# Token lists of a gated MoE kernel: list values from two broadcast instructions a group, and the shared expert's add to X moved ahead of the low halves

## The chip, the cores and the metric

The kernel runs on one core of a Trainium2 chip. A core has five engines that run their own instruction streams and meet only at semaphores: TensorE (PE in the profile, its weight loads PEld), VectorE (DVE), ScalarE (ACT), GpSimd (POOL), and SyncE (SP), which here only issues DMAs. The metric is the device time of one execution in microseconds; lower is better. Before the change it is 693.31 us, the median of three runs (689.36, 693.31 and 694.84).

## The reference, cut to what matters

```python
x = x + tanh(g_xattn[0]) * (0.6 * sigmoid(si + sj + b) + 0.4 * layernorm(x))   # si, sj from ctx_512
h = layernorm(x)                                     # 2048 tokens of 512
probs = softmax(h @ gate_w.T)                        # 16 experts
vals, idx = top_k(probs, 4)                          # each token goes to 4 experts
w = vals / sum(vals)
act = silu(h @ w_gate[e]) * (h @ w_up[e])            # fp4 codes times scales, 512 -> 2 x 384
out = sum over the 4 experts of w[e] * (act @ w_down[e])      # 384 -> 512
out = out + shared expert's (swiglu, down) on every token
x = x + tanh(g_ffn[0]) * out
```

## The kernel before, in words

The 2048 tokens are 16 tiles of 128 (NT = 16). The program has three stages. In the first the attention-like part, the two layer norms and the transposes make `xT`, the normalised tokens in two f16 halves. In the second, which lasts from about 45 to 186 us, the shared expert runs over the 16 tiles, one **shared slot** per tile, and beside it the routing is worked out. In the third the 16 routed experts run over lists of tokens that are gathered by indirect DMA, and the results are added to the output by indirect DMA.

**One shared slot i.** PE multiplies tile i by the gate and up weights in two halves of 12 matmuls (`gate_up`, L1203); between them it transposes the activations of slot i-1 (`transpose_act`, L1217); then it multiplies those by the down weights (`down`, L1231, 9 matmuls, slot i-1). ACT applies silu (L613) when both halves of slot i are there. DVE multiplies gate and up (`activations`, L989). ACT rounds the result to f16 (the high half, L620). DVE subtracts that from the f32 result (the low half, `low_halves`, L994); PE's next `transpose_act` waits for both halves. `add_y` (L998) adds the down result of slot i-1 from PSUM to X and frees that PSUM bank; it waits for `down(i-1)`. After that DVE does the slot's share of other work (`after_shared_slot`, L1029): dequantisation of the first routed expert (slots 5 to 8, L908 to L931), the routing (`route`, slot 9), ranks and positions (slot 10), token weights (slot 11), the lists (slots 11 and 12, `mark`), `lists` (slot 13), tables (slot 14), and the rest of the first routed expert's dequantisation (slot 15), which begins with the tick of L948 that lets PE start the first routed slot.

**The lists.** A token's j-th choice (j = 0 to 3) has a position in the list of its expert: a row (0 to 127) and a slot (0 to 79, since SLOTS = 80). `mark(j)` builds two f16 operands. `onehot` [128 tokens, 128 rows, 16 tiles] is 1 where the row matches, from one instruction of 2048 elements a partition (L1026). `values` [128 tokens, 16 tiles, 80 slots] is token number + 1 where the slot matches, and 0 elsewhere, from 16 instructions of 80 elements (L1023), one for each tile: compare `slot_h` (0 to 79) with the token's slot, multiply by the token's number. `list_tokens(j)` on PE then multiplies the two, 16 matmuls for each j, with `onehot[:, j % 2, :, i]` as the weights and the tile's `values` as the moving operand of 80 columns (L1258). All 64 matmuls add up in one PSUM bank. `values` and `onehot` have two buffers, so `mark(2)` waits for the end of `list_tokens(0)`, and `mark(3)` for that of `list_tokens(1)`.

**Order.** Every engine's order is that of the code. On PE the four `list_tokens` stand after `down(11)` (j = 0, 1) and after `down(12)` (j = 2, 3); behind them stand `gate_up(13)` and `gate_up(14)`. POOL makes constants at the start (L411 to L431), then helps with the layer norms, makes `place` (L489), and is idle until the lists are done.

Of the kernel before, what the change touches and what calls it, by code (L numbers as in the profile page):

```python
# [6 lines left out]
F32, F16 = mybir.dt.float32, mybir.dt.float16  # L7
I32, U16 = mybir.dt.int32, mybir.dt.uint16
ALU = mybir.AluOpType
# [3 lines left out]
P = 128  # L13
LN_EPS = 1e-5
P_ASEM = 0.6
TOP_K = 4
# [13 lines left out]
def gated_xattn_moe(nc, x, ctx_512, g_xattn, g_ffn, xattn_w, xattn_b, gate_w, gu_packed, gu_scales,  # L30
# [6 lines left out]
    NT = B * S // P  # L37
# [11 lines left out]
    SLOTS = T * TOP_K // P + E  # L49
# [15 lines left out]
    with ExitStack() as ctx:  # L65
        def sb(name, shape, dt):
            return ctx.enter_context(nc.sbuf_tensor(name, shape, dt))
# [4 lines left out]
        def sem(name):  # L72
# [80 lines left out]

        onehot = room_a[:, :].bitcast(F16).rearrange("p (b q i) -> p b q i", b=2, i=NT)
        values = mix_room[:, 1:3].rearrange("p k b h -> p (k b h)").bitcast(F16)[:, 0:2 * SLOTS * NT]\
            .rearrange("p (b i s) -> p b i s", b=2, i=NT)
        place = spare.rearrange("p b h -> p (b h)").bitcast(F16).rearrange("p (q i) -> p q i", i=NT)
        xg = room_b[:, 0:2 * ROW].rearrange("p (b n) -> p b n", b=2)
        at = [2 * ROW]
# [16 lines left out]
        rank = wide[:, E * NT:2 * E * NT].rearrange("p (e i) -> p e i", i=NT)  # L176
        g_pos = wide[:, 2 * E * NT:3 * E * NT].rearrange("p (i e) -> p i e", e=E)
        pos_i = sb("pos_i", [P, 3, TOP_K, NT], I32)
        pos_slot = sb("pos_slot", [P, TOP_K, NT], F32)
        pos_row = sb("pos_row", [P, TOP_K, NT], F16)  # L180
        start_f = sb("start_f", [P, E], F32)
        tri = sb("tri", [P, P], F16)
        ones16 = sb("ones16", [P, P], F16)
        sel16 = sb("sel16", [P, NT * E], F16)
        sel = sel16[:, :].rearrange("p (t e) -> p t e", e=E)
        token1 = sb("token1", [P, NT], F32)
        dump_row = sb("dump_row", [P, 1], F32)


# [7 lines left out]
        first_tiles_i = sb("first_tiles_i", [P, E], I32)  # L197
        pairs_i = sb("pairs_i", [P, 1], I32)
        slot_f = sb("slot_f", [P, SLOTS], F32)
        slot_h = sb("slot_h", [P, SLOTS], F16)  # L200
        before_s = sb("before_s", [P, SLOTS], F32)
        first_of_expert = sb("first_of_expert", [P, SLOTS], F32)
        slot_i = sb("slot_i", [P, SLOTS], I32)
# [122 lines left out]

            return 16 * LOADS * (n // 2 + 1)

        POOL_CONST = 16


        LEAD = 8
# [77 lines left out]
        def _(pool):  # L410
# [7 lines left out]
            nc.gpsimd.memset(ones16[:, :], 1.0).then_inc(pool_const, 1)  # L418
            for dst, pattern, base, mult in ((token1[:, :], [[P, NT]], 1, 1), (dump_row[:, :], [[0, 1]], DUMP + 1, 1),
                                             (iota_s[:, :], [[1, SLOTS]], 0, 0),  # L420
                                             (before_s[:, :], [[16, SLOTS // 2], [16, 2]], 0, 0),
                                             (slot_h[:, :], [[1, SLOTS]], 0, 0)):
                nc.gpsimd.iota(dst, pattern, base=base, channel_multiplier=mult,
                               allow_small_or_imprecise_dtypes=True).then_inc(pool_const, 1)
            pool.wait_ge(pool_const, 13)

            nc.gpsimd.affine_select(out=tri[:, :], in_=tri[:, :], compare_op=ALU.is_gt, fill=-1.0, base=0,
                                    pattern=[[1, P]], channel_multiplier=-1).then_inc(pool_const, 1)
            for ident in (id32, id16):
                nc.gpsimd.affine_select(out=ident[:, :], in_=ident[:, :], compare_op=ALU.not_equal, fill=1.0,  # L430
                                        base=0, pattern=[[-1, P]], channel_multiplier=1).then_inc(pool_const, 1)  # L431

            def inverse_std(k, b):

# [259 lines left out]
        def _(v):  # L694
# [289 lines left out]
            def activations(s, b, weight):  # L984

                if not isinstance(s, int) or s >= 2:
                    v.wait_ge(at_done, s - 1)
                v.wait_ge(sg_done, s + 1)
                nc.vector.scalar_tensor_tensor(act[:, b, :], gu_ps[:, 2 + b, 0:I], weight, sg[:, b, :], ALU.mult,  # L989
                                               ALU.mult).then_inc(act_done, 1)  # L990

            def low_halves(s, b):
                v.wait_ge(ah_done, s + 1)
                nc.vector.tensor_tensor(acth[:, b, 1, :], act[:, b, :], acth[:, b, 0, :], ALU.subtract).then_inc(al_done, 1)  # L994
# [18 lines left out]
            def mark(j):  # L1013

                if j >= 2:
                    v.wait_ge(list_ready, j - 1)
                else:
                    v.wait_ge(place_ready, 1)
                    for k in range(ROWS_AHEAD):
                        v.wait_ge(st_rows[k], 16 * (NT // ROWS_AHEAD))  # L1020

                for i in range(NT):
                    mm = nc.vector.tensor_scalar(values[:, j % 2, i, :], slot_h[:, :], pos_slot[:, j, i:i + 1], token1[:, i:i + 1],  # L1023
                                                 ALU.is_equal, ALU.mult)
                mm.then_inc(values_ready, 1)
                nc.vector.tensor_tensor(onehot[:, j % 2], pos_row[:, j, :].unsqueeze(1).broadcast_to([P, P, NT]), place,  # L1026
                                        ALU.is_equal).then_inc(onehot_ready, 1)

            def after_shared_slot(i):  # L1029

# [51 lines left out]
            second_stats(1)  # L1082
            for i in range(2, NT):
                activations(i, i % 2, shared_w[:, 0:1])
                low_halves(i, i % 2)
                add_y(i - 1)
                after_shared_slot(i)

            def head(r, e):
# [54 lines left out]
        def _(pe):  # L1144
# [108 lines left out]
            def list_tokens(j):  # L1253

                pe.wait_ge(onehot_ready, j + 1)
                pe.wait_ge(values_ready, j + 1)
                for i in range(NT):
                    mm = nc.tensor.matmul(rt_ps[:, 0:SLOTS], onehot[:, j % 2, :, i], values[:, j % 2, i, :],  # L1258
                                          start=(j == 0 and i == 0), stop=(j == TOP_K - 1 and i == NT - 1))
                mm.then_inc(list_ready, 1)  # L1260

# [103 lines left out]
```

## Time and profile before

| | |
|---|---|
| three timed runs | 689.36, 693.31, 694.84 us (median 693.31) |
| profiled execution, first to last instruction (span) | 689.3 us; this is the only time recorded for it |
| PE busy | 622.6 us (90%) |
| PE weight loads busy | 375.9 us (55%) |
| DVE busy | 496.2 us (72%) |
| ACT busy | 325.8 us (47%) |
| POOL busy | 327.7 us (48%) |
| mean granted TensorE clock | 0.98 of full speed |

The busy shares are means over stages with different limits. The page cuts the span into 40 slices of 17.2 us; PE's busy digits lie between 3 and 9 in the first thirteen slices, and are 9 (90% or more) in all later ones but the last. DVE's digits are 8 or 9 in the slices from 86.2 to 172.3 us, the end of which is the stretch in which the lists are made. A chain of waits is read from its end backwards: each piece was released by the one before it.

### The profile page before, as it was taken

Reading aid. Unit: us, or ns where it says so; the run is one execution under the profiler, and the core shown is the slowest. Engines: PE = TensorE matmul, PEld = TensorE weight load, DVE = VectorE, ACT = ScalarE, POOL = GpSimd, SP = SyncE. Lnnn points to the kernel's source line nnn. Section 1 sums busy time; section 2 is a strip of 40 time slices with the busy share of each in tenths; the row PEclk is TensorE's granted clock in tenths of the full one; section 3 lists DMA queues with packets and bytes.
Section 4 is the critical chain, followed back from the end, with each engine's and each line's share of the span. In section 5 each row is a group of like instructions: output and inputs, shape, how many; then the busy total and the mean of one; then the engine's idle time right before and its main releaser. Section 6 shows DMA issues by size and latency. Waiting matters only on the chain.

```text
span 689.3 us, 17258 instructions
## 1 busy us (share of the span) xinstructions
PE 622.6 (90%) x4394; PEld 375.9 (55%) x4395; DVE 496.2 (72%) x1271; ACT 325.8 (47%) x558; POOL 327.7 (48%) x506
## 2 busy tenths in 40 slices
PE   3668869887898999999999999999999999999992
PEld 2444545444554656565555656566565655656550
DVE  5878788989776858588777867688588878867210
ACT  1763577231343554454544455454554545455441
POOL 2521844000235456564646565564655656565432
PEclk9999989998999999999999999999999999999996
DMA  8670111128156875857577684848767587654432
GB/s 235 203 241 1 63 46 70 40 53 276 49 162 152 207 179 118 189 115 189 107 196 174 128 215 82 225 78 204 177 127 186 117 193 174 141 89 68 90 47 31
DMA packets 49841, 93.72 MB, mean 136 GB/s; under 512 B 8840, under 2 KB 16776, under 8 KB 49816
## 3 DMA queue, kind: packets, MB, share of 16 engines
q0 software_dynamic: 16128, 38.35, 30.1%
q1 hardware_dynamic: 32936, 55.04, 27.1%
q8 instruction: 11, 0.18, 0.1%
q10 hardware_dynamic: 752, 0.04, 0.1%
q14 instruction: 14, 0.11, 0.1%
HBM read 65.16 MB, written 28.24 MB: 135 GB/s over the span
## 4 chain that ended last, share of the span: by engine, by line
PE 72%; DVE 13%; ACT 4%; DMA 3%; issue 3%; POOL 2%; SPq 1%; DVEq 0%; POOLq 0%; ACTq 0%
PE gu_ps L1203 41%; PE bank L1231 20%; PE bank L1243 4%; PE bank L1217 4%; DVE mix_room L1023 2%; DMA dn_sc<-dn_scale_halves 2%; DVE act L989 1%; DMA room_a<-in_ctx 1%; ACT acth L620 1%; PE gu_ps L1163 1%; DVE X L998 1%; PE bank L1160 1%; DVE acth L994 1%; DVE dn_code L920 1%; ACT mix_room L579 1%
## 5 line engine op out<-in xcount | busy, mean ns | idle before, releaser
L1203 PE MATMUL gu_ps<-wgu,mix_room 128*128 x1728 | 304.4, 326 | 3.3 <-DVE tick L948 2.1
L1203 PEld LDWEIGHTS gu_ps<-wgu,mix_room 128*128 128x128 f16 x1728 | 166.0, 98 | 114.5 <-issue 7.4
L1231 PE MATMUL bank<-wdn,aT 128*128 (+1 forms) x792 | 186.5, 381 | 4.2 <-ACT aT L627 3.7
L528 POOL DMA_INDIRECT out<-mix_room,idx_s x72 | 123.9, 1721 | 31.9 <-issue 30.5
L627 ACT ACTIVATE aT<-bank 128x768 f16<-128x768 f16 x88 | 71.2, 810 | 130.9 <-PE bank L1217 126.0
L1231 PEld LDWEIGHTS bank<-wdn,aT 128*128 128x128 f16 x792 | 77.6, 98 | 89.5 <-issue 3.2
L989 DVE SCALAR_TENSOR_TENSOR act<-gu_ps,wslot,sg x72 | 44.5, 618 | 96.2 <-ACT sg L613 79.4
L499 POOL TENSOR_TENSOR pool_tick<-ones 128x1 f32<-128x1 f32 x144 | 36.0, 250 | 162.7 <-DMA out<-mix_room,idx_s 79.6
L620 ACT ACTIVATE acth<-act 128x384 f16<-128x384 f32 x88 | 46.0, 523 | 135.8 <-DVE act L989 131.4
L510 POOL DMA_INDIRECT room_b<-token_rows,idx_g x72 | 76.5, 1063 | 12.1 <-issue 3.7
L994 DVE TENSOR_TENSOR acth<-act,acth (+1 forms) x88 | 49.2, 560 | 38.1 <-ACT acth L620 37.6
L507 POOL COPY idx_g<-room_b 128x1 int32 (+1 forms) x72 | 41.8, 581 | 70.9 <-DVE tick L859 51.3
L638 ACT ACTIVATE mix_room<-bank 128x1024 f16<-128x1024 f16 x72 | 73.2, 1017 | 0.3 <-PE bank L1243 0.3
L925 DVE TENSOR_TENSOR wgu<-dq_code,gu_sc 128x768 f16<-128x768 f16 x136 | 70.8, 561 | 2.3
L1203 PE MATMUL gu_ps<-wgu,xT 128*128 128x384 f16 x384 | 71.5, 340 | 0.0
L613 ACT ACTIVATE sg<-gu_ps 128x384 f32<-128x384 f32 x88 | 43.2, 491 | 57.3 <-PE gu_ps L1203 55.0
L1217 PE MATMUL bank<-id,acth 128*128 128x128 f16 x528 | 44.0, 219 | 10.7 <-ACT acth L620 8.7
L1203 PEld LDWEIGHTS gu_ps<-wgu,xT 128*128 128x128 f16 x384 | 37.4, 101 | 25.5 <-issue 5.0
L1217 PEld LDWEIGHTS bank<-id,acth 128*128 128x128 f16 x528 | 36.1, 98 | 25.4 <-ACT acth L620 13.8
L931 DVE TENSOR_TENSOR wdn<-dn_code,dn_sc 128x384 f16<-128x384 f16 x136 | 43.6, 362 | 0.7
L1243 PE MATMUL bank<-id,room_b 128*128 128x128 f16 x576 | 43.9, 219 | 0.0
L644 ACT ACTIVATE mix_room<-bank 128x512 f32<-128x512 f32 x72 | 41.8, 580 | 4.2 <-PE bank L1231 4.2
(156 smaller groups left out, 586.2 us busy)
## 6 DMA issues: line engine op xcount, KB each, us to landing
dn_sc<-dn_scale_halves SPq DMA_DIRECT2D x34, 384.0 KB
dn_raw<-in_L_ffn_down_packed SPq DMA_DIRECT2D x48, 256.0 KB
gu_sc<-gu_scale_halves SPq DMA_DIRECT2D x34, 192.0 KB
X<-in_x SPq DMA_DIRECT2D x4, 1024.0 KB, 8.1
token_rows<-room_a SPq DMA_DIRECT2D x16, 256.0 KB, 2.3
out<-X SPq DMA_DIRECT2D x4, 1024.0 KB, 10.6
gu_raw<-in_L_ffn_gate_up_packed SPq DMA_DIRECT2D x16, 192.0 KB
gu_raw<-in_L_ffn_gate_up_packed SPq DMA_DIRECT2D x16, 191.9 KB
```

The lines of the kernel that those rows point to most:

```text
L510: nc.gpsimd.indirect_dma_start(xg[:, b, :], None, rows_dram[:, :], bass.IndirectOffsetOnAxis(idx_g[:, b:b + 1], 0)).then_inc(xg_ld[b], 16)
L528: nc.gpsimd.indirect_dma_start(out[:, :], bass.IndirectOffsetOnAxis(idx_s[:, b:b + 1], 0), y_sb[:, b, :], None, compute_op=ALU.add).then_i ...
L620: nc.scalar.activation(acth[:, b, 0, :], act[:, b, :], ACT.Copy).then_inc(ah_done, 1)
L627: nc.scalar.activation(aT[:, b].rearrange("p a c t -> p (a c t)"), at_ps, ACT.Copy).then_inc(aT_done, 1)
L638: nc.scalar.activation(xTs[:, b, :], xT_ps, ACT.Copy).then_inc(xTs_done, 1)
L925: link(nc.vector.tensor_tensor(wgu[:, buf, hl, c, :], dq_code[:, :], gu_sc[:, buf, hl, :], ALU.mult), wait=False)
L989: nc.vector.scalar_tensor_tensor(act[:, b, :], gu_ps[:, 2 + b, 0:I], weight, sg[:, b, :], ALU.mult, ALU.mult).then_inc(act_done, 1)
L994: nc.vector.tensor_tensor(acth[:, b, 1, :], act[:, b, :], acth[:, b, 0, :], ALU.subtract).then_inc(al_done, 1)
L1203: mm = nc.tensor.matmul(ps[b][:, 0:I], x(xp * HC + c), wgu[:, w, wp, c, col:col + I], start=(c == 0 and xp == 0 and wp == 0), stop=(c == H ...
L1217: mm = nc.tensor.transpose(at_ps[:, k * P:(k + 1) * P], acth[:, b, hl, t * P:(t + 1) * P], id16[:, :])
L1231: mm = nc.tensor.matmul(y_ps[0 if shared else b][:, :], aT[:, b, ap, t, :], wdn[:, w, wp, t, :], start=(n == 0), stop=(n == 3 * IC - 1))
L1243: mm = nc.tensor.transpose(xT_ps[:, k * P:(k + 1) * P], chunk_h(halves[:, k // HC, :], k % HC), id16[:, :])
```

## The change

Three things change. First, `values` is laid out as [tokens, slots, tiles] in place of [tokens, tiles, slots], and is built by two wide instructions on DVE in place of 16 narrow ones: a compare of 1280 elements a partition (`pos_slot` broadcast over the slots against a constant `slot_place`), then `onehot` as before, then a multiply of 1280 elements in place by `token1` broadcast over the slots. All operands are f16; `pos_slot` and `token1` were f32. The multiply is now what signals `values_ready`. Second, POOL makes the constant `slot_place` (1280 elements a partition) once, behind its other constants, in place of `slot_h` (80 elements); the first `mark` waits for it too. Third, in shared slots 2 to 15 `add_y(i - 1)` stands between `activations(i)` and `low_halves(i)`, where it stood behind `low_halves(i)`. PE's matmuls of the lists are the same in number and shape, but a moving operand `values[:, j % 2, :, i]` now takes every 16th f16 element (32 bytes apart), where it took 80 neighbours.

```diff
--- before.py
+++ after.py
@@ -153,7 +153,7 @@
 
         onehot = room_a[:, :].bitcast(F16).rearrange("p (b q i) -> p b q i", b=2, i=NT)
         values = mix_room[:, 1:3].rearrange("p k b h -> p (k b h)").bitcast(F16)[:, 0:2 * SLOTS * NT]\
-            .rearrange("p (b i s) -> p b i s", b=2, i=NT)
+            .rearrange("p (b s i) -> p b s i", b=2, i=NT)
         place = spare.rearrange("p b h -> p (b h)").bitcast(F16).rearrange("p (q i) -> p q i", i=NT)
         xg = room_b[:, 0:2 * ROW].rearrange("p (b n) -> p b n", b=2)
         at = [2 * ROW]
@@ -176,14 +176,15 @@
         rank = wide[:, E * NT:2 * E * NT].rearrange("p (e i) -> p e i", i=NT)
         g_pos = wide[:, 2 * E * NT:3 * E * NT].rearrange("p (i e) -> p i e", e=E)
         pos_i = sb("pos_i", [P, 3, TOP_K, NT], I32)
-        pos_slot = sb("pos_slot", [P, TOP_K, NT], F32)
+        pos_slot = sb("pos_slot", [P, TOP_K, NT], F16)
+        slot_place = sb("slot_place", [P, SLOTS, NT], F16)
         pos_row = sb("pos_row", [P, TOP_K, NT], F16)
         start_f = sb("start_f", [P, E], F32)
         tri = sb("tri", [P, P], F16)
         ones16 = sb("ones16", [P, P], F16)
         sel16 = sb("sel16", [P, NT * E], F16)
         sel = sel16[:, :].rearrange("p (t e) -> p t e", e=E)
-        token1 = sb("token1", [P, NT], F32)
+        token1 = sb("token1", [P, NT], F16)
         dump_row = sb("dump_row", [P, 1], F32)
 
 
@@ -197,7 +198,6 @@
         first_tiles_i = sb("first_tiles_i", [P, E], I32)
         pairs_i = sb("pairs_i", [P, 1], I32)
         slot_f = sb("slot_f", [P, SLOTS], F32)
-        slot_h = sb("slot_h", [P, SLOTS], F16)
         before_s = sb("before_s", [P, SLOTS], F32)
         first_of_expert = sb("first_of_expert", [P, SLOTS], F32)
         slot_i = sb("slot_i", [P, SLOTS], I32)
@@ -326,7 +326,7 @@
 
             return 16 * LOADS * (n // 2 + 1)
 
-        POOL_CONST = 16
+        POOL_CONST = 15
 
 
         LEAD = 8
@@ -418,17 +418,19 @@
             nc.gpsimd.memset(ones16[:, :], 1.0).then_inc(pool_const, 1)
             for dst, pattern, base, mult in ((token1[:, :], [[P, NT]], 1, 1), (dump_row[:, :], [[0, 1]], DUMP + 1, 1),
                                              (iota_s[:, :], [[1, SLOTS]], 0, 0),
-                                             (before_s[:, :], [[16, SLOTS // 2], [16, 2]], 0, 0),
-                                             (slot_h[:, :], [[1, SLOTS]], 0, 0)):
+                                             (before_s[:, :], [[16, SLOTS // 2], [16, 2]], 0, 0)):
                 nc.gpsimd.iota(dst, pattern, base=base, channel_multiplier=mult,
                                allow_small_or_imprecise_dtypes=True).then_inc(pool_const, 1)
-            pool.wait_ge(pool_const, 13)
+            pool.wait_ge(pool_const, 12)
 
             nc.gpsimd.affine_select(out=tri[:, :], in_=tri[:, :], compare_op=ALU.is_gt, fill=-1.0, base=0,
                                     pattern=[[1, P]], channel_multiplier=-1).then_inc(pool_const, 1)
             for ident in (id32, id16):
                 nc.gpsimd.affine_select(out=ident[:, :], in_=ident[:, :], compare_op=ALU.not_equal, fill=1.0,
                                         base=0, pattern=[[-1, P]], channel_multiplier=1).then_inc(pool_const, 1)
+
+            nc.gpsimd.iota(slot_place[:, :, :], [[1, SLOTS], [0, NT]], base=0, channel_multiplier=0,
+                           allow_small_or_imprecise_dtypes=True).then_inc(place_ready, 1)
 
             def inverse_std(k, b):
 
@@ -1015,16 +1017,18 @@
                 if j >= 2:
                     v.wait_ge(list_ready, j - 1)
                 else:
-                    v.wait_ge(place_ready, 1)
+                    v.wait_ge(place_ready, 2)
                     for k in range(ROWS_AHEAD):
                         v.wait_ge(st_rows[k], 16 * (NT // ROWS_AHEAD))
 
-                for i in range(NT):
-                    mm = nc.vector.tensor_scalar(values[:, j % 2, i, :], slot_h[:, :], pos_slot[:, j, i:i + 1], token1[:, i:i + 1],
-                                                 ALU.is_equal, ALU.mult)
-                mm.then_inc(values_ready, 1)
+                by_slot = [P, SLOTS, NT]
+                step(nc.vector.tensor_tensor(values[:, j % 2], pos_slot[:, j, :].unsqueeze(1).broadcast_to(by_slot),
+                                             slot_place[:, :, :], ALU.is_equal), wait=False)
                 nc.vector.tensor_tensor(onehot[:, j % 2], pos_row[:, j, :].unsqueeze(1).broadcast_to([P, P, NT]), place,
                                         ALU.is_equal).then_inc(onehot_ready, 1)
+                v.wait_ge(vs, count[0])
+                nc.vector.tensor_tensor(values[:, j % 2], token1[:, :].unsqueeze(1).broadcast_to(by_slot), values[:, j % 2],
+                                        ALU.mult).then_inc(values_ready, 1)
 
             def after_shared_slot(i):
 
@@ -1082,8 +1086,8 @@
             second_stats(1)
             for i in range(2, NT):
                 activations(i, i % 2, shared_w[:, 0:1])
+                add_y(i - 1)
                 low_halves(i, i % 2)
-                add_y(i - 1)
                 after_shared_slot(i)
 
             def head(r, e):
@@ -1255,7 +1259,7 @@
                 pe.wait_ge(onehot_ready, j + 1)
                 pe.wait_ge(values_ready, j + 1)
                 for i in range(NT):
-                    mm = nc.tensor.matmul(rt_ps[:, 0:SLOTS], onehot[:, j % 2, :, i], values[:, j % 2, i, :],
+                    mm = nc.tensor.matmul(rt_ps[:, 0:SLOTS], onehot[:, j % 2, :, i], values[:, j % 2, :, i],
                                           start=(j == 0 and i == 0), stop=(j == TOP_K - 1 and i == NT - 1))
                 mm.then_inc(list_ready, 1)
 
```

DVE's order around slot 11, where the first two lists are made, was this (`mix_room` holds `values` and `place`, `room_a` holds `onehot`, `acth` the two halves, `X<-bank` is `add_y`):

```order
L989 SCALAR_TENSOR_TENSOR act<-gu_ps,shared_w,sg 128x384
L994 TENSOR_TENSOR acth<-act,acth 128x384
L998 SCALAR_TENSOR_TENSOR X<-bank,X 128x512
L788 TENSOR_TENSOR r_exp<-r_exp,sel 128x256
L789 TENSOR_REDUCE r_sum<-r_exp 128x16
L790 RECIPROCAL r_sum<-r_sum 128x16
L792 TENSOR_SCALAR r_sum<-r_sum,shared_w 128x16
L793 TENSOR_TENSOR cw<-r_exp,r_sum 128x256
L1023 TENSOR_SCALAR mix_room<-slot_h,pos_slot,token 128x80 x16
L1026 TENSOR_TENSOR room_a<-pos_row,mix_room 128x2048
```

In the changed program, whose lines are numbered two to four higher there, the same place reads:

```order
L991 SCALAR_TENSOR_TENSOR act<-gu_ps,shared_w,sg 128x384
L1000 SCALAR_TENSOR_TENSOR X<-bank,X 128x512
L996 TENSOR_TENSOR acth<-act,acth 128x384
L790 TENSOR_TENSOR r_exp<-r_exp,sel 128x256
L791 TENSOR_REDUCE r_sum<-r_exp 128x16
L792 RECIPROCAL r_sum<-r_sum 128x16
L794 TENSOR_SCALAR r_sum<-r_sum,shared_w 128x16
L795 TENSOR_TENSOR cw<-r_exp,r_sum 128x256
L1025 TENSOR_TENSOR mix_room<-pos_slot,slot_place 128x1280
L1027 TENSOR_TENSOR room_a<-pos_row,mix_room 128x2048
L1030 TENSOR_TENSOR mix_room<-token,mix_room 128x1280
```

The add to X moved ahead of the low half, 16 narrow instructions became one ahead of `onehot` and one behind it, and the last of the three is now the multiply; the same three stand for each of the four j.

On POOL, at the end of its constants and ahead of its first work for a layer norm (`rstd`), the program before had:

```order
L423 IOTA before_s 128x80
L423 IOTA slot_h 128x80
L427 AFFINE_SELECT tri<-tri 128x128
L430 AFFINE_SELECT id<-id 128x128 x2
L437 TENSOR_TENSOR rstd<-veps,mhalf 128x4
```

and the changed one has:

```order
L422 IOTA before_s 128x80
L426 AFFINE_SELECT tri<-tri 128x128
L429 AFFINE_SELECT id<-id 128x128 x2
L432 IOTA slot_place 128x1280
L439 TENSOR_TENSOR rstd<-veps,mhalf 128x4
```

The small `slot_h` went, and the wide `slot_place` stands behind the last constant that another engine waits for.

## Rows read from the trace of the kernel before

**Rows 1.** The page, chain that ended last: shares of the span by engine
```profile
PE 72%; DVE 13%; ACT 4%; DMA 3%; issue 3%; POOL 2%; SPq 1%; DVEq 0%; POOLq 0%; ACTq 0%
```

**Rows 2.** Stretches: length; PE, PEld, DVE, ACT, POOL busy; PE clock; DMA share; GB/s
```profile
149.00:157.00 8.00, 3.99 (x31) 2.25 (x28) 7.95 (x33) 0.49 (x1) 0.00 (x0) 1.00 0.72 166
157.00:164.00 7.00, 5.21 (x33) 3.14 (x33) 6.41 (x22) 0.53 (x1) 0.00 (x0) 0.51 0.96 297
```

**Rows 3.** Chain of waits, 145 to 190 us: start, length, what
```profile
161.01 3.37 DVE mix_room L1023 x16
164.38 1.13 DVE room_a L1026
...
170.07 1.19 PE bank L1258 x16
171.26 1.95 PE gu_ps L1203 x12
...
186.16 2.12 PE gu_ps L1203 x12
```

**Rows 4.** Timeline of DVE: start, length, instruction, count, idle before and its releaser
```profile
119.54 2.65 DVE L920 TENSOR_SCALAR dn_code<-dn_bits 128x384 f16<-128x384 f16 x1
...
128.49 1.03 DVE L925 TENSOR_TENSOR wgu<-dq_code,gu_sc 128x768 f16<-128x768 f16 x2
...
146.75 0.56 DVE L994 TENSOR_TENSOR acth<-act,acth 128x384 f16<-128x384 f32 x1 [0.59 <-ACT acth L620]
147.23 0.68 DVE L998 SCALAR_TENSOR_TENSOR X<-bank,X 128x512 f32<-128x512 f32 x1
...
149.63 3.46 DVE L1023 TENSOR_SCALAR mix_room<-slot_h,pos_slot,token 128x80 f16<-128x80 f16 x16
...
176.13 0.62 DVE L989 SCALAR_TENSOR_TENSOR act<-gu_ps,shared_w,sg 128x384 f32<-128x384 f32 x1 [3.00 <-ACT sg L613]
...
179.50 1.49 DVE L841 TENSOR_TENSOR room_b<-iota_s,cum_f 128x1280 f16<-128x1280 f32 x1
```

**Rows 5.** Timeline of PE, slots 10 to 14
```profile
137.63 0.62 PE L1249 MATMUL bank<-sel,tri 128*128 128x256 f16 x1 [1.30 <-DVE sel L782]
138.07 0.64 PE L1250 MATMUL bank<-sel,ones 128*128 128x256 f16 x1
138.53 2.13 PE L1203 MATMUL gu_ps<-wgu,xT 128*128 128x384 f16 x12
...
149.69 2.10 PE L1231 MATMUL bank<-wdn,aT 128*128 128x512 f16 x9
154.28 1.19 PE L1258 MATMUL bank<-mix_room,room_a 128*128 128x80 f16 x16 [2.48 <-DVE room_a L1026]
158.79 1.28 PE L1258 MATMUL bank<-mix_room,room_a 128*128 128x80 f16 x16 [3.32 <-DVE room_a L1026]
159.87 4.04 PE L1203 MATMUL gu_ps<-wgu,xT 128*128 128x384 f16 x12
...
175.33 2.11 PE L1231 MATMUL bank<-wdn,aT 128*128 128x512 f16 x9
```

**Rows 6.** Weight loads of lines L1258 and L1249: ns min/median/max, first and last start
```profile
L1258 PEld LDWEIGHTS bank<-mix_room,room_a x64: 140/164/178, 154.3 to 171.0; 128*128 128x128 f16 x64
L1249 PEld LDWEIGHTS bank<-sel,tri x1: 95/95/95, 137.6 to 137.6; 128*128 128x128 f16 x1
```

**Rows 7.** Timeline of POOL
```profile
14.64 1.06 POOL L437 TENSOR_TENSOR rstd<-veps,mhalf 128x4 f32<-128x4 f32 x1 [10.70 <-DVE veps L726]
...
119.36 2.62 POOL L489 IOTA mix_room<- 128x2048 f16 x1
```

**Rows 8.** Chain of waits, 74 to 90 us
```profile
76.95 0.60 DVE X L998
...
78.28 4.60 POOL X L443 x4
```

**Rows 9.** Chain of waits, 195 to 222 us
```profile
204.83 11.53 DMA dn_sc<-dn_scale_halves
```

## The prediction

> **What bounds the kernel now.** I read the chain of waits first. Over the span PE carries 72% of it and DVE 13% [rows 1]; the reader is to see where those 13% lie, since nothing that the change edits is PE's own work. Between 145 and 190 us the chain runs on DVE through the narrow instructions of the lists and `onehot` (16 take 3.37 us, then 1.13), and reaches PE only behind the last list at 170.07 [rows 3]. The stretches agree: from 149 to 157 us DVE is busy 7.95 of 8.00 us and PE 3.99 [rows 2]. DVE's timeline shows the other idle time: in a shared slot it waits 0.59 us for ACT's high half ahead of the low half [rows 4]. After 175.33 the chain is `gate_up(14)`, then DVE's tables and the tick that lets PE begin the first routed slot at 186.16 [rows 3, 5]. What the change gains or loses must show in that start; whatever moves it moves the rest of the program with it.
>
> **Before the lists: `add_y` ahead of the low half.** The wait of 0.59 us is filled by an add of 0.60 (147.23 in [rows 4], less overlap), provided that `down(i-1)` is done. Then DVE leaves a slot about 0.6 us earlier, while the low half ends where it did. This counts only where DVE sets the pace, which is in slots 7 to 11 and 15 (by slot 14 it waits 3.00 us for PE). In slot 7, dequantisation behind it is held up by POOL: an instruction there lasts 2.65 from 119.54, while POOL makes `place` from 119.36 to 121.98 [rows 4, 7]. I count 0.2 of its 0.6. Slots 8, 9, 10 and 11 count 0.6 each. In slot 3 the add is on the chain too (76.95), ahead of the layer norm's factors and POOL's work from 78.28 [rows 8]; there `down(2)` ends late, and I take 0.4. Slots 2, 4, 5 and 6 wait for PE or POOL next, and count nothing. So the low half of slot 11 comes 0.4 + 0.2 + 3 x 0.6 = 2.4 us earlier, and the first `mark` 3.0 us earlier (0.6 of slot 11 more).
>
> **The lists on DVE.** The trace has no compare of 1280 elements with these operands. `onehot` has the same form (f16, one operand broadcast over the middle dimension), and takes 1.13 us for 2048 [rows 3]; a plain f16 multiply of 768 takes 1.03 - 0.56 = 0.47 [rows 4]. The line through both is 0.07 + 0.516 ns an element, so 0.73 us for 1280. The bounds are 0.70 (1280/2048 of `onehot`) and 1.50 (an f32 operand, 179.50 [rows 4]); 0.73 is taken, since the types are `onehot`'s. A `mark` becomes 0.73 + 1.13 + 0.73 = 2.60 us against 3.37 + 1.13 = 4.50, which is 1.9 less, 7.6 for four. The wait between compare and multiply is covered by `onehot`, which is between them.
>
> **The lists on PE.** These matmuls took 68 ns each (158.79 to 159.87, 16 of them [rows 5]). That is about the weight load: on L1258, whose weights lie 32 bytes apart, it lasts 164 ns against 95 for neighbouring ones [rows 6]. The 80 neighbouring columns hid behind it. Now these lie 32 bytes apart too. One place of the trace streams such an operand, L1249 and L1250, whose moving `sel` has that step: 256 columns take 0.44 and 0.46 us from start to start [rows 5], or 1.72 to 1.80 ns a column, at full clock. A plain stream of 384 columns takes 1.95/12 us, 0.42 ns a column [rows 3]. So 80 columns cost 138 to 144 ns, and with a start of a few ns I take 142 ns, 2.27 us a list. Bounds: 1.08 as now, and 16 x (142 + 68) = 3.4 if weight load and stream add up.
>
> The Trainium skill speaks against the new layout here: "SBUF — State Buffer", section "Door 1: The DMA port swizzle", has lines of 16 bytes and a penalty for each access that goes to a new line, which every column now does; the slow `sel` agrees. The Trainium skill's "TensorE: Matmul & The Clock Gate", section "Part 2: What happens when you issue a matmul", gives weights and stream a read port each; by that the 3.4 would not occur.
>
> **The sum.** A row of PE's timeline has a pipeline tail of 0.17 us (2.13 against 1.95 for the same 12 matmuls [rows 3, 5]), which is left out here. PE ended `down(11)` at 149.69 + 2.10 - 0.17 = 151.62, and now does so 2.4 earlier, at 149.2, since the slot's transposes waited for the low half. `mark(0)` runs from 146.6 to 149.2, so list 0 takes PE from 149.4 to 151.7; `mark(1)` ends at 151.8, list 1 takes from 151.9 to 154.2. From here PE is the one that is waited for: `gate_up(13)` with its transposes takes 175.33 - (171.26 - 0.17) = 4.24, as `gate_up(14)` does there, `down(12)` 1.94, lists 2 and 3 take 4.54, `gate_up(14)` again 4.24, and ends at 169.15. Marks 2 and 3 end by 156.2 and 158.8 and delay nothing. Before, `gate_up(14)` ended at 175.33 [rows 5]: **6.2 us earlier**. Of 7.6 us that DVE saves in the lists, and 3.0 ahead of them, 4.4 is given back because PE becomes the bound and its lists are 4.8 us longer. In slot 14 the add must wait for `down(13)`, so the low half and the tables come 0.2 later after the activation than before; slot 15 gains its 0.6, as `down(14)` is done by then. **6.2 - 0.2 + 0.6 = 6.6 us**; the first routed slot starts at 179.6.
>
> At nothing I cost: `slot_place` on POOL, some 1.7 us by 2.62 x 1280/2048, under an idle stretch of 10.70 us that ends at 14.64 [rows 7]; with that cover gone it would cost the 1.7. Nor do I cost the f16 forms of `pos_slot` and `token1`, made by the instructions that made them in f32. The gather of the first routed rows keeps its lead, since `lists`, which it waits for, comes 7 us earlier too. Nothing behind 186 us gains by itself. The next wait there, 11.53 us for a scale load [rows 9], hangs on a store behind the last `add_y`, in expert 0's stream, and moves along.
>
> The profiled execution has 689.3 us and becomes 682.7. It is 0.6% below the median of the timed runs, which spread by 5.5 us. Against the median the forecast is 693.3 - 6.6 = **686.7 us**.
>
> **The rivals.**
>
> *The strided stream costs nothing* (0.10). Lists stay at 1.1 us: list 1 ends at 153.0, `down(12)` at 159.2, list 3 at 161.4, `gate_up(14)` at 165.7. That is 9.6 and with slots 14 and 15 10.0 us, so 683.3. For it: the matmuls are short and wait on weights anyway. Against it: `sel` at 1.75 ns a column. The Trainium skill's "TensorE: Matmul & The Clock Gate", section "Back-to-back issue gap", lets the gap grow with the column count alone, and would give this case; the `sel` rows disagree with it.
>
> *Stream and weight load add up* (0.13). Lists of 3.4 us cost 4 x 1.13 more, less 0.3 that PE waited ahead of list 1: 6.6 - 4.2 = 2.4 us gain, 690.9. For it is that both would then read with long steps at once; the rows of `sel`, whose weights are neighbours, do not tell.
>
> *The clock falls in the lists* (0.12). Before, PE idled ahead of lists 0 and 1 (2.48 and 3.32 us), the clock was at 0.51 from 157 to 164 us, the lower of 1.2 and 2.4 GHz, and a half of `gate_up(13)` took 4.04 instead of 1.95 us [rows 2, 5]. DVE hid that then. If it falls again behind lists 0 and 1, 2.0 us of it now lie on PE's path: 4.6 us gain, 688.7. Against it: the idle times are down to 0.2.
>
> *The broadcast instructions run no faster than the f32 form* (0.03): 1.50 us each, a `mark` 4.13. List 1 then starts 3.1 us later and PE's path behind it with it, for a gain of 3.5 and 689.8. Against it: `onehot`.
>
> *Slower* (0.04). The stream and the clock meet: at the lower clock the strided columns cost twice 1.75 ns, 280 ns, and add the weight load's 68, 5.6 us a list. Four lists cost 4 x 3.3 = 13.2 more than I take, against 6.6: slower by 6.6, and with the half of `gate_up(13)` by 8.6, about 702. It decides from 3.9 us a list on. Against it: at the lower clock list 1 took 1.28 us against list 0's 1.19 [rows 5], so strided reads hardly follow that clock.
>
> **How the numbers follow.** The forecast has 0.58. A measurement tells about 1% of this kernel, 6.9 us, from no change, and the forecast of 6.6 lies just inside, so the spread of the runs splits it: 0.32 of the 0.58 faster by more, as the median shown is above the profiled execution and the lowest run and may fall back, 0.25 within, 0.01 slower. The free stream adds 0.09 faster, the clock 0.03, the rest 0.01, together 0.45; the slow case leaves 0.03 slower, 0.04 in all; 0.51 are within. The range takes in the free stream with 1.9 us of run spread below it, and the adding stream above: 681.5 to 691.
>
> **What the changed profile would show.** Compare and multiply of 1280 at 0.73 us from start to start; 16 list matmuls in 2.3 us; no idle time of 0.59 ahead of the low half in slots 7 to 11; `gate_up(13)` at full clock; PE's first routed slot at 179.6 us, and its distance to the end unchanged at 503.1 us. Wrong I am if list matmuls keep to 68 ns or go above 200, if the clock falls under `gate_up(13)`, or if the distance to the end changes.

## The result: 5% slower, and the loss lies where the prediction said nothing changes

The changed kernel took 725.75 us (median of 6, 722.01 to 730.66) against 691.38 us for the kernel before (median of 6: the three runs of the table and three more): a ratio of 1.0497, 95% interval 1.0455 to 1.0539. The forecast was 686.7 us and its range ended at 691. The profiled execution took 722.01 us, its span is 720.2 us; the prediction made the span 682.7. The 37.5 us between the two split at the first routed slot. PE starts it at 185.14 us where 179.6 was forecast (5.5 us), and from there to the end are 535.1 us where 503.1 was forecast (32.0 us).

**The lists.** Below is PE's timeline of the changed kernel (start, time, engine, line, operation, tiles, shapes, count, idle time before it), with rows in between left out. It answers to [rows 5]:

```profile
149.06 2.10 PE L1235 MATMUL bank<-wdn,aT 128*128 128x512 f16 x9
151.24 5.24 PE L1262 MATMUL bank<-mix_room,room_a 128*128 128x80 f16 x32
156.30 3.61 PE L1207 MATMUL gu_ps<-wgu,xT 128*128 128x384 f16 x12
163.98 5.05 PE L1262 MATMUL bank<-mix_room,room_a 128*128 128x80 f16 x32
168.84 3.34 PE L1207 MATMUL gu_ps<-wgu,xT 128*128 128x384 f16 x12
174.77 2.11 PE L1235 MATMUL bank<-wdn,aT 128*128 128x512 f16 x9
185.14 2.12 PE L1207 MATMUL gu_ps<-wgu,mix_room 128*128 x12 [1.64 <-DVE tick L950]
```

From start to start the two pairs of lists take 5.06 and 4.86 us, so 158 and 152 ns a matmul. PE no longer waits for DVE ahead of them, but the first half of `gate_up` behind each pair takes 3.61 and 3.34 us instead of the 2.11 of full clock; the kernel before lost that behind its first pair (4.04 [rows 5]), and not behind its second (2.12 from 171.09). The stretches of the same run give the clock (busy us and count of each engine, granted clock, DMA share, GB/s); they answer to [rows 2]:

```profile
149.00:157.00 8.00, 7.93 (x46) 5.76 (x44) 8.00 (x11) 1.02 (x2) 0.00 (x0) 0.93 0.83 197
157.00:164.00 7.00, 7.00 (x39) 3.75 (x38) 4.21 (x6) 1.81 (x3) 0.00 (x0) 0.83 1.00 366
164.00:169.00 5.00, 5.00 (x34) 4.77 (x33) 1.16 (x2) 0.02 (x1) 0.00 (x0) 1.00 0.72 281
169.00:176.00 7.00, 7.00 (x37) 3.96 (x35) 1.23 (x5) 1.30 (x2) 3.04 (x6) 0.76 0.35 96
```

The granted clock falls behind both pairs, to the lower of its two levels for a part of the stretch, although PE was busy for 26.93 of these 27 us.

DVE's side went as forecast. Its timeline:

```profile
148.40 0.82 DVE L1025 TENSOR_TENSOR mix_room<-pos_slot,slot_place 128x1280 f16<-128x1280 f16 x1
149.14 1.22 DVE L1027 TENSOR_TENSOR room_a<-pos_row,mix_room 128x2048 f16<-128x2048 f16 x1
150.27 0.82 DVE L1030 TENSOR_TENSOR mix_room<-token,mix_room 128x1280 f16<-128x1280 f16 x1
151.01 0.82 DVE L1025 TENSOR_TENSOR mix_room<-pos_slot,slot_place 128x1280 f16<-128x1280 f16 x1
```

Compare and multiply take 0.74 us from start to start, a `mark` 151.01 - 148.40 = 2.61 us.

**The routed stage.** The change edits nothing there, and yet DVE's loop over pairs of experts (a `Fori` of six passes) now stops at each of its five jumps back. This is the chain of waits of the changed kernel around the first stop (start, us, what, with small pieces left out; "issue" is time in which the engine waited for nothing that the profile shows, and DVEq is DVE's sequencer):

```profile
315.99 0.55 DVE wgu L927
316.54 3.71 issue
320.25 0.07 DVEq L1141
320.36 0.33 DVEq L1106
321.13 0.05 issue
321.84 0.63 DVE act L991
322.49 0.53 ACT acth L622
323.86 0.80 PE bank L1221 x6
```

L1141 is the loop itself: the last multiply of a pass is done at 316.54, and the jump back to the loop's first instruction shows only at 320.25. The next activation waits, ACT waits for it, and PE waits for ACT. The chain has five such pieces, 3.71, 3.33, 5.69, 6.32 and 4.25 us, at 316.54, 376.27, 447.31, 513.64 and 576.96. DVE's idle time ahead of the activation behind them is 5.30, 4.91, 7.29, 7.91 and 5.84, together 31.25 us. At the same five jumps the kernel before has 1.02, 1.22, 1.86, 1.72 and 1.21, together 7.03; this is its first:

```profile
317.85 0.62 DVE L989 SCALAR_TENSOR_TENSOR act<-gu_ps,wslot,sg  x1 [1.02 <-issue]
```

So DVE's idle time grew by 24.2 of the 32.0 us. The other 7.8 are not split by a run, but the stretches say where they can lie: PE idles during a stop, and in the 6 to 8 us behind the five stops the granted clock is 0.79, 0.60, 0.72, 0.51 and 0.55, where it is 1.00 behind all five jumps of the kernel before. These are the 8 us behind the first stop, in the changed kernel and then in the kernel before:

```profile
322.00:330.00 8.00, 6.14 (x36) 3.85 (x37) 6.08 (x16) 3.62 (x7) 3.93 (x6) 0.79 0.82 197
```

```profile
322.00:330.00 8.00, 8.00 (x55) 4.63 (x54) 6.55 (x17) 3.88 (x8) 2.46 (x7) 1.00 0.77 195
```

The page has one more difference, in the DMA queue that brings instructions (packets, MB, share of the engines' span), here of the changed kernel and then of the kernel before:

```profile
q14 instruction: 39, 0.32, 0.1%
```

```profile
q14 instruction: 14, 0.11, 0.1%
```

The extra 25 packets, five for each jump, are the only hint on the page at what DVE waits for. The trace says more, stretch by stretch: exactly one packet of this queue falls into each of the five stops, and in the kernel before none at all falls between 303 and 620 us, in which its five jumps lie.

### The profile page after: what moved, and what is told of

Its sections match the earlier page's. It is cut to its first block, busy times and chain, and to the rows that moved or that the text cites. A ratio compares the mean times of both kernels' runs of the same rounds, so it can differ in the third digit from the quotient of the medians.

```text
span 720.2 us, 17202 instructions
## 1 busy us (share of the span) xinstructions
PE 639.7 (89%) x4394; PEld 387.4 (54%) x4395; DVE 488.1 (68%) x1215; ACT 325.8 (45%) x558; POOL 326.1 (45%) x506
## 4 chain that ended last, share of the span: by engine, by line
PE 69%; DVE 10%; issue 7%; ACT 4%; DMA 3%; POOL 2%; DVEq 2%; SPq 1%; ACTq 0%; POOLq 0%
PE gu_ps L1207 38%; PE bank L1235 18%; PE bank L1247 4%; PE bank L1221 4%; DMA dn_sc<-dn_scale_halves 2%; DVE act L991 2%; PE bank L1262 1%; ACT acth L622 1%; DMA room_a<-in_ctx 1%; PE gu_ps L1167 1%; POOL room_a L462 1%; PE bank L1164 1%; PE bank L1191 1%; DVE wgu L927 1%; DVEq L991 1%
## 5 line engine op out<-in xcount | busy, mean ns | idle before, releaser
L1207 PE MATMUL gu_ps<-wgu,mix_room 128*128 x1728 | 310.6, 330 | 2.6 <-DVE tick L950 1.6
L1207 PEld LDWEIGHTS gu_ps<-wgu,mix_room 128*128 128x128 f16 x1728 | 168.3, 99 | 117.5 <-issue 12.3
L1221 PE MATMUL bank<-id,acth 128*128 128x128 f16 x528 | 45.7, 225 | 32.8 <-ACT acth L622 31.0
L1207 PE MATMUL gu_ps<-wgu,xT 128*128 128x384 f16 x384 | 74.1, 348 | 0.0
L509 POOL COPY idx_g<-room_b 128x1 int32 (+1 forms) x72 | 37.4, 520 | 68.9 <-DVE tick L861 47.1
L1247 PE MATMUL bank<-id,room_b 128*128 128x128 f16 x576 | 46.2, 225 | 0.0
```

The lines of the kernel that those rows point to most:

```text
L1207: mm = nc.tensor.matmul(ps[b][:, 0:I], x(xp * HC + c), wgu[:, w, wp, c, col:col + I], start=(c == 0 and xp == 0 and wp == 0), stop=(c == H ...
L1221: mm = nc.tensor.transpose(at_ps[:, k * P:(k + 1) * P], acth[:, b, hl, t * P:(t + 1) * P], id16[:, :])
L1247: mm = nc.tensor.transpose(xT_ps[:, k * P:(k + 1) * P], chunk_h(halves[:, k // HC, :], k % HC), id16[:, :])
```

## The experiments

Theory 1: the change took 56 instructions out of DVE's program ahead of the loop (16 narrow ones became 2 wide ones, four times; the page counts 1271 and now 1215), so the loop lies at another place of the code, and the jump back now leads to code that must be fetched again. Theory 2: the moved add, the strided lists or the data's timing slow the routed stage. The kernel has a knob that moves DVE's code: `LEAD` small memsets at the start of DVE's program, 8 of them, while DVE waits for the scales. Their tile is the last that is laid out, so no other tile's address moves with it. Each ratio below is to executions of the kernel before that were timed beside the run.

**1. The changed kernel with the 56 instructions put back as memsets.**

```diff
-        LEAD = 8
+        LEAD = 64
```

> The changed kernel with 64 instead of 8 small memsets at the start of VectorE's program, in the time in which it waits for the scales (8 of them took 0.26 us, so 56 more are 1.8 us inside an idle 4.9 us). From the marks on, every VectorE instruction of the program then stands at the same place of the code as in the kernel before, because the change took 56 instructions out ahead of it. Theory 1 (the place of VectorE's expert loop in its code costs the 32 us): no issue pieces of 3 us or more in the chain, first routed slot at about 185 us, from there to the end 503 us (kernel before) and not 535, time 688 to 692. Theory 2 (the order of the add to X, the strided lists or the later data slow the routed stage): the 535 us stay, time 722 to 728. If part of each, something between.

Measured: 689.98 us, ratio to the kernel before 0.9976 (0.9954 to 0.9997). First routed slot at 184.47 us, 504.0 us from there, 14 packets. The whole loss of the routed stage is gone with nothing of the change's own work undone: theory 1 holds, theory 2 falls.

**2. The kernel before with its loop moved to where the change puts it** (`LEAD = 208`; 200 more is 56 fewer modulo 256).

> The kernel before with 208 instead of 8 memsets at VectorE's start: 200 more instructions, which is 56 fewer modulo 256, and nothing else. Theory 1 with blocks of 256 instructions: the expert loop falls across its blocks as in the changed kernel, the routed stage goes from 503 to about 535 us, and the memsets end about 2 us after the scales landed, so 720 to 727 us, with issue pieces of 3 to 6 us at the loop's back edge. Theory 2: only the late start, 691 to 694 us, no such pieces. Theory 1 with another period than 256 could give either; then a second point would be needed.

Measured: 728.64 us, 1.0562 (1.0512 to 1.0611); 538.9 us behind the first routed slot, 41 packets, the five pieces in the chain again (3.00 to 6.14 us). The loss needs nothing of the change but the place.

**3. The kernel before with 256 more** (`LEAD = 264`), against the doubt that it is the number of memsets.

> The kernel before with 264 memsets at VectorE's start, 256 more than it has, beside the run with 200 more that took 728 us. If the place counts modulo 256 instructions, the routed stage is back at 503 us with about 14 packets of the instruction queue, and the time is 690 plus 3 to 4 us of late start: 692 to 696 us. If it is the number of memsets or the later start that cost the 38 us of the run with 200 more, 730 us or above.

Measured: 692.91 us, 1.0017 (0.9993 to 1.0041); 503.5 us behind the first routed slot, 16 packets. A place 256 instructions further is as free as the old one; more memsets than in run 2 cost nothing but the later start (first routed slot 191.08, in a profiled execution that was the slowest of the eight).

**4. Half the padding** (`LEAD = 36` in the changed kernel).

> The changed kernel with 36 memsets at VectorE's start: halfway between the changed kernel (8, routed stage 535 us) and the run with 64 (504 us). By the theory of the code's place there is one edge between them and the time is one of the two, 725 or 690 us, with 39 or 14 packets of the instruction queue; a cost that falls with the number of instructions would give some 707 us.

Measured: 747.75 us, 1.0816 (1.0771 to 1.0862), which neither expectation had: 563.2 us behind the first routed slot. Its chain shows why (small pieces left out):

```profile
315.65 4.94 issue
320.59 0.07 DVEq L1141
320.70 0.33 DVEq L1106
321.37 0.11 DVEq L1095
321.47 5.62 issue
327.09 0.05 DVEq L989
```

Each pass has two stops: one at the jump, and a second 5 instructions later (L1141, three of L1106, L1095), between L1095 and L989. I read it so: the loop's first 5 instructions lie at the very end of one piece of code, and the next piece has to come too. In the changed kernel, with 28 memsets fewer, 33 instructions lie ahead of that edge, and no second stop shows. With pieces of 128, which run 5 suggests and run 6 tests, this gives the edge's place: the loop's start is 123 instructions into a piece of 128 here, by which it is at 95 in the changed kernel and at 23 in the kernel before.

**5. Sixty further than the good place** (on the kernel of run 9, which stands at 23 too; `LEAD = 124`).

> The kernel with groups of 4 tiles with 124 memsets instead of 64 at VectorE's start, 60 more instructions ahead of the loop. The kernel before stood less than 28 instructions from the place where the loop begins to cost (the run with 36 memsets took 748 us); if the loop only has to lie inside two blocks of 256, its 332 instructions leave 180 places that are all alike, and 60 further on the routed stage is 501 to 505 us as at 64, about 14 packets of the instruction queue, time 683 to 687. If each place has its own price, the routed stage moves by several us either way.

Measured: 719.5 us, 1.0420 (1.0388 to 1.0452); 538.3 us behind the first routed slot, 40 packets, five pieces in the chain of 3.13 to 6.92 us. My first form of theory 1, that the loop must only lie inside two blocks of 256, fell here. The instruction queue's packets (0.32 MB in 39, 8.2 KB each) suggested smaller pieces. The Trainium skill's "Runtime: NRT & Kernel Launch", section "Instruction fetch mechanics", has 256 instructions in 16 KiB, by which a packet would hold 128, an estimate.

**6 and 7. Two models of the pieces** (`LEAD = 192` and `LEAD = 88` on the same kernel).

> The kernel with groups of 4 tiles with 192 memsets, 128 more than the run of 684.5 us; the run with 60 more took 719.5 us, so that lying inside two blocks of 256 instructions is not enough. Model H: the code is held in pieces of 128 instructions (the instruction queue's packets are about 8 KB), four of them, one ahead of the running one; the jump back costs when its target lies more than two pieces behind. Then 128 more instructions change nothing: routed stage 501 to 505 us, about 14 packets, time 684 to 688 with a start that is up to 2 us later. Model B: blocks of 256, the next one fetched from halfway on, so that the jump back costs when it stands in the second half of a block: 128 more put it there, routed stage about 535 us, time 718 to 724.

> The kernel with groups of 4 tiles with 88 memsets, 24 more than the run of 684.5 us and 36 fewer than the run of 719.5. In the run with 36 memsets the second stall comes 5 instructions behind the loop's start, which sets the piece's edge there; by it the loop's start is at 23 of its piece of 128 at 64 memsets, at 47 here, and the jump back 331 instructions later is still in the third piece (47 + 331 = 378, below 384). By both models no loss: 683 to 687 us, about 14 packets. If the edge was read wrongly: about 719.

Measured: 682.89 us, 0.9900 (0.9858 to 0.9941), 501.4 us behind the first routed slot, 15 packets; and 685.77 us, 0.9936 (0.9848 to 1.0023), 505.2 us, 15 packets. Model H held, model B fell. Five packets a jump fit it as well: the changed kernel's loop reaches over four pieces (95 + 331 = 426), and one is fetched ahead of the running one; in the kernel before, whose loop reaches over three, nothing was fetched again. DVE's timeline at the start of the run with 192 memsets shows the same 128: it pauses after 60 memsets, and again after 128 more.

```profile
0.86 1.72 DVE L707 MEMSET lead<- 128x1 f16 x60 [0.71 <-PEq L1358]
2.98 3.63 DVE L707 MEMSET lead<- 128x1 f16 x128 [0.40 <-issue]
7.14 0.15 DVE L707 MEMSET lead<- 128x1 f16 x4 [0.53 <-issue]
```

All places together. The loop has 332 instructions in the compiled program (the traces have only those that ran), the jump is 331 behind its start, and by model H it is free while start + 331 stays below 3 x 128 = 384:

| place of the loop's start in its piece | + 331 | runs | behind the first routed slot, us |
|---|---|---|---|
| 23 | 354 | kernel before, runs 1, 3, 6, 8 to 12 | 501.4 to 505.7 |
| 47 | 378 | run 7 | 505.2 |
| 83 | 414 | run 5 | 538.3 |
| 95 | 426 | changed kernel, run 2 | 535.1, 538.9 |
| 123 | 454 | run 4 | 563.2 |

The same section of the Trainium skill's "Runtime: NRT & Kernel Launch" says that a taken branch to a target outside the window of two pages of 256 instructions stops the engine for a fetch. The kind of stop is what the traces show; the size of the window differs. Whichever of the edges found here begins a page of 256, either the changed kernel's loop or run 5's would lie within two pages, and both stop at each jump. The measurement decides: three pieces of 128 fit all runs here, with the limit itself seen only as between 378 and 414.

**8. The moved add alone** (on the kernel before).

```diff
-                low_halves(i, i % 2)
                 add_y(i - 1)
+                low_halves(i, i % 2)
```

> The kernel before with the shared slots' add to X moved between the activations and their low part, nothing else; VectorE's number of instructions and the places of its loop do not change. My sum for this part alone was 3.0 us at the first mark; the changed kernel's trace showed waits of 0.72 us for the down product in five slots, so 0 to 3 us here: first routed slot 183 to 186.5 us, time 688 to 692. Theory 1: from the first routed slot to the end 503 us. Theory 2 in the form that the order of the add slows the routed stage: 520 us or more, time above 705.

Measured: 688.22 us, 0.9962 (0.9940 to 0.9984): 2.6 us of gain by the ratio (1.1 to 4.1). First routed slot at 180.86 in a profiled execution that was the fastest of ten.

**9. The change with a step of 8 bytes on PE**: values in four groups of 4 tiles, the same two wide instructions.

```diff
-            .rearrange("p (b s i) -> p b s i", b=2, i=NT)
+            .rearrange("p (b g s i) -> p b g s i", b=2, g=NT // 4, i=4)
...
-                    mm = nc.tensor.matmul(rt_ps[:, 0:SLOTS], onehot[:, j % 2, :, i], values[:, j % 2, :, i],
+                    mm = nc.tensor.matmul(rt_ps[:, 0:SLOTS], onehot[:, j % 2, :, i], values[:, j % 2, i // 4, :, i % 4],
```

(`LEAD = 64`; the broadcast views of the two instructions follow the layout, and `slot_place` keeps 4 columns a slot.)

> The run with 64 memsets and the moved add, with the list values laid out in four groups of 4 tiles, slot by slot inside a group, so that TensorE's moving operand steps 4 values (8 bytes) and not 16 (32 bytes); the same two wide VectorE instructions. If the step of the moving operand is what makes a list matmul take 155 ns: 68 to 80 ns each as in the kernel before, the lists then wait for the marks (2.61 us each), the pairs end about 1.3 and 2.7 us earlier, and the clock after them holds better; first routed slot at 178 to 181 us against 184.5, time 683 to 687. If the weight load (140 to 178 ns, unchanged here) sets the pace once VectorE no longer does, the matmuls stay at 140 to 165 ns, first routed slot at 184 to 185 us, time about 690. If the wide instructions lose VectorE's speed with 4 values in a row: marks of 3.5 us or more and no gain.

Measured: 684.46 us, 0.9906 (0.9879 to 0.9933), the fastest here but for run 6, which was executed twice. PE's timeline, with rows in between left out:

```profile
152.40 1.42 PE L1262 MATMUL bank<-mix_room,room_a 128*128 128x80 f16 x16
155.01 1.44 PE L1262 MATMUL bank<-mix_room,room_a 128*128 128x80 f16 x16 [1.19 <-DVE mix_room L1030]
156.28 2.13 PE L1207 MATMUL gu_ps<-wgu,xT 128*128 128x384 f16 x12
162.47 2.69 PE L1262 MATMUL bank<-mix_room,room_a 128*128 128x80 f16 x32
164.98 2.13 PE L1207 MATMUL gu_ps<-wgu,xT 128*128 128x384 f16 x12
179.60 2.12 PE L1207 MATMUL gu_ps<-wgu,mix_room 128*128 x12 [1.63 <-DVE tick L950]
```

From start to start 32 matmuls take 2.51 us, 78 ns each, and both halves of `gate_up` behind the lists run at full clock (granted 1.00 from 149 to 187 us). That full clock does not come with the layout: with the same lists the half behind the first pair took 3.81, 3.81 and 4.02 us in the profiled executions of runs 5, 7 and 12, and 2.13 in run 6's. Behind the second pair it took 2.13 in all five. DVE's wide instructions stay at 0.82 us. Weights with their step of 32 bytes are as in the changed kernel, so it was the moving operand that set its pace.

**10. The same with groups of 8 tiles**, a step of 16 bytes.

> As the kernel with groups of 4, with two groups of 8 tiles: the moving operand steps 8 values (16 bytes). It places the price between a step of 2 bytes (68 ns a matmul) and 32 bytes (155 ns). A price that grows with the step: about 85 to 110 ns; a price that is there or not: 68 or 155 ns. Time between the run with groups of 4 and 690 us.

Measured: 688.96 us, 0.9969 (0.9947 to 0.9991). PE's timeline, with rows in between left out:

```profile
150.63 5.17 PE L1262 MATMUL bank<-mix_room,room_a 128*128 128x80 f16 x32
155.62 3.81 PE L1207 MATMUL gu_ps<-wgu,xT 128*128 128x384 f16 x12
163.49 4.94 PE L1262 MATMUL bank<-mix_room,room_a 128*128 128x80 f16 x32
168.25 2.13 PE L1207 MATMUL gu_ps<-wgu,xT 128*128 128x384 f16 x12
```

156 and 149 ns a matmul, about the same as at 32 bytes: the price is there or not, with its edge between 8 and 16 bytes. The clock fell behind the first pair only.

**11 and 12. The lists without the moved add**, at 32 bytes (changed kernel, `LEAD = 64`, the diff of run 8 reversed) and at 8 bytes (run 9, likewise).

> The changed kernel with 64 memsets at VectorE's start and with the add to X back behind the low part: the two wide instructions and the strided lists alone, with the code of VectorE's loop where it stood before. Theory 1: 503 us behind the first routed slot. Against the run with 64 memsets and the moved add it gives the price of the move: by the changed kernel's trace 0.6 us at the end of down(11), by my sum 3.0; so first routed slot at 185.5 to 188 us, time 688 to 694. Theory 2 in the form that the strided lists slow the routed stage: above 715.

> The kernel with groups of 4 tiles with the add to X back behind the low part. The move alone on the kernel before gave -2.2 us of the medians (ratio 0.9962), the whole 6.7 (0.9906). If the two add up, this takes 686 to 688 us; if the lists only gain when the low part comes earlier, about 690; if the moved add is worth nothing here, 684 to 685.

Measured: 692.63 us, 1.0032 (1.0004 to 1.0060), a loss of 2.2 us (0.3 to 4.1); and 687.33 us, 0.9943 (0.9923 to 0.9963), a gain of 3.9. With the moved add the two were 0.9976 and 0.9906, so it is worth 0.56% and 0.37% there, and 0.38% in run 8.

## Why the prediction was wrong, step by step

- **"Nothing behind 186 us gains by itself", the "distance to the end unchanged at 503.1 us": this step failed.** It asked what the change's data and waits do to the routed stage, and found nothing; that is right, as run 1 shows. It did not ask what 56 instructions fewer do to the code behind them. The chain and the timeline of before could not show it, since the loop stood at a free place there (23; by model H it stays free up to 52). The change moved it to 95. DVE's idle time at the five jumps grew from 7.0 to 31.3 us, and the clock fell behind each: together the distance to the end grew by 32.0 us, 32.0 of the 37.5 us of the miss. The rival that ended slower, a list of 5.6 us at the lower clock, was another mechanism; strided lists took 2.4 to 2.5 us each.
- **The `mark`s** were right: 2.60 us forecast, 2.61 measured, with 0.74 for each wide instruction where the line through two rows gave 0.73. `slot_place` on POOL took 1.60 us and is hidden, as costed.
- **The lists on PE** were mis-sized. Their step was right in kind (the moving operand's step, read off `sel`), but 142 ns came out as 152 to 158, and two lists of 4.54 us as 4.86 and 5.06.
- **The clock** was a rival at 0.12, "the clock falls in the lists", argued away because the idle times were gone. In the profiled execution it came true behind both pairs without idle time: 1.50 and 1.23 us more for two halves of `gate_up`, which with the lists' 0.8 make 3.6 of the 5.5 us lost ahead of the first routed slot. Another 1.8 is that list 0 began at 151.24 us and not at 149.4, since `down(11)` came 0.6 us earlier than before (149.06 against 149.69) and not 2.4. Single executions tell little here: in the nine profiled ones with the moved add `down(11)` began between 146.06 and 150.23 us, and the clock fell behind the first pair in all profiled executions of this case but those of runs 6 and 9, and behind the second only at 32 bytes, in three of four. Runs 11 and 12 weigh it all by the medians: marks and lists at 32 bytes lose 2.2 us, where the forecast's share for them was a gain of 3.2 (6.6 less the moved add's 3.4); at 8 bytes they gain 3.9.
- **The moved add** was forecast at 3.4 us (3.0 at the first mark, 0.6 - 0.2 in slots 14 and 15) and gave 2.6 (run 8; 1.1 to 4.1). The size was right; the way was not as told slot by slot, which is luck in part: the add was to fill DVE's idle time ahead of the low half, but in the changed kernel the add itself waits for the down product, as the waits from 60 to 136 us show (us, times, longest):

```profile
DVE act L991 <- ACT sg L615: 6.6, 5, 3.5
DVE X L1000 <- PE bank L1235: 3.9, 5, 1.1
```

- So with the loop at its old place the change is worth 0.24% (0.03 to 0.46), 1.7 us where 6.6 were forecast, a quarter. Its 689.98 us would have been inside the range only because that reached up to 691.

What stays open: why the clock falls behind some lists and not behind others is not told by these runs, nor why a stop lasts 3.0 us at one jump and 6.9 at another; and where between 378 and 414 the limit of model H lies was not measured.

## What to carry to other kernels

An edit that adds or removes instructions ahead of a loop also moves the loop in its engine's code; count the loop's instructions and its place, compare the instruction queue's packets of the two profiles, and look for "issue" at the line of the loop before blaming the edit's own work. A few idle instructions at the start put it back. Where values are laid out for a wide VectorE instruction, keep the step of what TensorE then streams small (8 bytes here): grouping by four kept both engines fast.

## What the runs showed of the hardware

- A jump back over 331 instructions on DVE left 1.0 to 1.9 us of idle time in the kernel before, or stopped its chain for 3.0 to 6.9 us, by where the loop stood; at one place a second stop of 4.1 to 6.0 us followed it 5 instructions later. One packet of 8.2 KB of the instruction queue lies in each stop of the changed kernel. Moving a free loop by 128 or by 256 instructions left it free, and all runs fit pieces of 128, of which the loop may reach over three.
- Behind the five stops the granted clock was 0.51 to 0.79, where it was 1.00 at the same jumps of the kernel before.
- A list matmul of 80 columns, f16, took 68 ns at a step of 2 bytes [rows 5], 78 at 8, 149 to 156 at 16 and 152 to 158 at 32, with the same weights.
- The granted clock fell to 0.83 and 0.76 in stretches behind the changed kernel's lists though PE was busy 7.93 of the 8.00 us in which the first pair ran. With the step of 8 bytes it stayed at 1.00 in run 9, with PE busy 6.74 of the same 8.00, and fell behind the first pair in three of the other four runs at that step.
